# Softmax denominators moved behind V, part of the causal mask moved to TensorE, earlier row maxima and shorter reciprocals in a two-layer transformer kernel

## What is computed

```python
x = x + _L0_attn_ref(_layernorm(x), wq, wk, wv, wo)      # 32 query heads, 8 key/value heads, width 32
x = x + _L0_ffn_ref(_layernorm(x), ...)                  # stream mixing with Sinkhorn
x = x + _L1_attn_ref(_layernorm(x), Wq, Wk, Wv, Wo)      # the same sizes, another rotary order
x = x + _L1_ffn_ref(_layernorm(x), ...)                  # base matrix and experts

# attention:
q = rope(x @ wq); k = rope(x @ wk); v = x @ wv           # each key head serves 4 query heads
scores = q k^T / sqrt(32) + causal mask                  # per head 1024 x 1024
out = softmax(scores) @ v
return out @ wo
```

## Time and profile before

| | |
|---|---|
| median of 3 runs | 3118.09 us (3112.07 to 3120.93) |
| the profiled execution | 3121.41 us, of which its span is 3119.7 us |
| TensorE matmul busy | 2780.3 us, 89% |
| TensorE weight load busy | 1788.4 us, 57% |
| VectorE busy | 1933.4 us, 62% |
| ScalarE busy | 1001.4 us, 32% |
| GpSimd busy | 715.2 us, 23% |
| mean granted clock of TensorE | 0.945 of 2.4 GHz |

### The profile page before, as it was taken

How to read it: one execution, slowest core, us unless ns; L and a number is a source line. 1 busy time by engine, 2 the same in 40 slices (tenths; PEclk the granted TensorE clock), 3 DMA queues, 4 the chain that set the end, 5 groups by cost and what they waited for, 6 DMA issues and landing times. The chain is left out here.

```text
span 3119.7 us, 49191 instructions
## 1 busy us (share of the span) xinstructions
PE 2780.3 (89%) x15824; PEld 1788.4 (57%) x15824; DVE 1933.4 (62%) x4357; ACT 1001.4 (32%) x1549; POOL 715.2 (23%) x693
## 2 busy tenths in 40 slices
PE   7899998999999799652859999989999996997999
PEld 5545554655554488652646455436555542885887
DVE  4577777557777433588765677775677774324543
ACT  2143435134343411352521443433244344101000
POOL 6223231433231000000044323214223220001111
PEclk8999999999999899765979999989999998998999
DMA  3323222323131422000123323223323221443111
GB/s 139 102 64 89 70 72 72 113 73 97 56 102 30 140 81 67 0 0 0 81 115 105 101 63 89 69 64 110 94 63 97 58 77 73 158 135 148 68 67 41
DMA packets 121063, 252.84 MB, mean 81 GB/s; under 512 B 12720, under 2 KB 39728, under 8 KB 120880
## 3 DMA queue, kind: packets, MB, share of 16 engines
q1 hardware_dynamic: 120912, 251.03, 25.5%
HBM read 166.57 MB, written 84.41 MB: 80 GB/s over the span
## 5 line engine op out<-in xcount | busy, mean ns | idle before, releaser
L560 ACT ACTIVATE a_prob<-a_pst 128x1024 f32<-128x1024 f32 (+3 forms) x768 | 593.0, 814 | 726.2 <-PE a_pst L827 724.7
L647 DVE CUSTOM_DVE_ANT_0 a_psh<-a_psh,a_edge 128x128 f32<-128x128 f32 (+3 forms) x1024 | 487.6, 514 | 218.5 <-PE a_psh L780 208.1
L780 PE MATMUL a_psh<-a_kst,a_qst 127*128 127x512 f32 (+3 forms) x1536 | 511.7, 394 | 29.3 <-issue 12.0
L780 PEld LDWEIGHTS a_psh<-a_kst,a_qst 127*128 127x128 f32 x1536 | 255.9, 189 | 455.4 <-DVE a_mx L647 199.3
L827 PE MATMUL a_pst<-a_qst,a_kst 128*128 128x512 f32 (+2 forms) x1536 | 398.8, 361 | 28.9 <-ACT a_prob L560 11.0
L650 DVE TENSOR_REDUCE a_mx<-a_psh 128x1 f32<-128x512 f32 x512 | 343.6, 689 | 71.1 <-PE a_psh L780 65.1
L847 PE MATMUL a_ppv<-a_prob,a_vg 128*32 128x512 f32 (+3 forms) x3072 | 335.0, 508 | 15.6 <-POOL a_prob L464 10.6
L464 POOL TENSOR_SCALAR_AFFINE_SELECT a_prob<-a_prob 128x512 f32<-128x512 f32 x256 | 171.9, 672 | 759.4 <-ACT a_prob L560 758.2
L827 PEld LDWEIGHTS a_pst<-a_qst,a_kst 128*128 128x128 f32 x1536 | 267.1, 192 | 128.4 <-issue 56.2
L847 PE MATMUL a_pden<-a_prob,a_ones 128*32 128x512 f32 (+3 forms) x3072 | 332.0, 504 | 0.0
L691 DVE RECIPROCAL a_dens<-a_dens 128x512 f32<-128x512 f32 x64 | 214.6, 3353 | 75.6 <-ACT a_dens L568 66.4
(11 more groups left out here) (217 smaller groups left out, 3958.8 us busy)
## 6 DMA issues: line engine op xcount, KB each, us to landing
a_qst<-q SPq DMA_DIRECT2D x192, 256.0 KB, 4.5
a_wraw<-in_wqkv SPq DMA_DIRECT2D x52, 512.0 KB, 5.7
q<-a_stg_hi SPq DMA_DIRECT2D x64, 256.0 KB, 2.6
q<-a_stg_lo SPq DMA_DIRECT2D x64, 256.0 KB, 2.8
oT<-a_oT SPq DMA_DIRECT2D x64, 256.0 KB, 2.5
a_kst<-kT SPq DMA_DIRECT2D x96, 128.0 KB, 3.0
h_oraw<-oT SPq DMA_DIRECT2D x16, 512.0 KB, 4.1
h_x<-in_x SPq DMA_DIRECT2D x16, 512.0 KB, 4.7
```

The lines of the kernel that those rows point to most:

```text
L560: act.activation(prob[k % 2][:, 2 * half:2 * half + 2, off:], pst[:, half, :, off:], ACT.Exp, scale=scale).then_inc(s["exp_done"], 1)
L647: part = dve.tensor_tensor_reduce(scores, scores, edge[:, BANK - n:], 1.0, 2 * MASKED, ALU.add, ALU.max, mx_hq[kc][:, h, qt:qt + 1])
L780: mm = pe.matmul(psh[:, at, i * n:(i + 1) * n], qst[par][0:P - 1, h, qt * P:(qt + 1) * P], kst[par][0:P - 1, kc * BANK:kc * BANK + n], sta ...
```

## The change

Six edits, all in the attention.

- `TOGETHER`: in the units 0, 1, 2, 3, 9, 10 and 11, what stood between `("PV", e, 0)` and `("PV", e, 1)` goes behind the latter, so that denominators follow V at once. A use `S` that was due after `("PV", e, 0)` of such a unit goes behind `("ST", e + 1, 1)`, that is, ahead of V.
- The window over which the uses `S` are spread gets two more places ahead: behind `("ST", 1, 1)` and behind `("PV", 0, 1)`. The first use so comes before V of unit 0, and before the last two pieces of the projection.
- Where a use on the diagonal holds more than one head (128 or 256 columns each), TensorE adds the mask with one more matmul per head: a bf16 identity times the last 128 columns of `edge`, accumulated on the scores. VectorE then takes one plain `tensor_reduce` for the whole bank. Uses of 384 and 512 columns stay with VectorE's masked maximum. That is 6 of 38 uses, with 16 matmuls more, per group and per prologue.
- `NORM`: in place of the reciprocal of 128 x 512, VectorE transposes `dens` in blocks of 32 x 32 into `oT[k]`, takes the reciprocal of one column of each block (128 x 16), and transposes that back, repeated, into `dens`. The wait for the store of `oT[k]` moves ahead of the first transpose.
- GpSimd makes the bf16 copy of the identity.
- GpSimd clears the padding of `kst` before the powers, and that of `qst` in eight parts between them.

```diff
+TOGETHER = (0, 1, 2, 3, 9, 10, 11)
...
-        window = [step for unit in steps[1:10] for step in unit]
+        window = [steps[0][1], steps[0][3]] + [step for unit in steps[1:10] for step in unit]
         total, done, k = sum(map(columns, window)), 0, 0
+        slot = {("PV", e, 0): ("ST", e + 1, 1) for e in TOGETHER}
         for step in window:
             done += columns(step)
             while k < len(USES) and k * total < done * len(USES) - total // 2:
-                after[step] += [("S", k)]
+                after[slot.get(step, step)] += [("S", k)]
                 k += 1
...
     order = [("ST", 0, 0), ("ST", 0, 1)] + ([("HI", 1), ("LO", 1), ("RS", 1)] if full_s else []) + first
+    for e in TOGETHER:
+        after["PV", e, 1][:0] = after["PV", e, 0]
+        after["PV", e, 0] = []
...
+        rden = sb("rden", [P, BANK // HD])
...
+            pool.drain()
+            pool.tensor_copy(identb[:, :], ident[:, :])
             pool.drain().then_inc(s["const"], 1)
...
-            for k in range(ST_):
-                reciprocal_deviation(k, k)
-                if k == 5:
-                    w_lo(0, 0)
-            pool.drain()
             for i in range(2):
                 pool.memset(kst[i][96:P, :].bitcast(F32), -1.0)
                 pool.drain()
                 pool.memset(kst[i][96:P - 1, :].bitcast(F32), 0.0)
                 pool.drain()
-                pool.memset(qst[i][96:P - 1, :, :].bitcast(F32), 0.0)
+            for k in range(ST_):
+                reciprocal_deviation(k, k)
+                if k == 5:
+                    w_lo(0, 0)
+                pool.drain()
+                pool.memset(qst[k // GH][96:P - 1, k % GH, :].bitcast(F32), 0.0)
                 pool.drain()
             pool.drain().then_inc(s["padded"], 1)
...
-                if last:
+                if last and m == 1:
...
                         dve.drain()
+                        dve.wait_ge(o_stored[k], DMA0 + n * 16)
+                        dve.sem_inc(s["dve_turn"], 1)
                         dve.wait_ge(s["acc_copied"], AC0 + 2 * q + 2)
-                        dve.reciprocal(dens[:, :], dens[:, :])
+                        dve.transpose(oT[k][:, :], dens[:, :])
                         dve.drain()
-
-                        dve.wait_ge(o_stored[k], DMA0 + n * 16)
+                        dve.reciprocal(rden[:, :], oT[k][:, :].rearrange("p (c r) -> p c r", r=HD)[:, :, 0])
+                        dve.drain()
+                        dve.transpose(dens[:, :], rden[:, :].unsqueeze(2).broadcast_to([P, BANK // HD, HD]))
+                        dve.drain()
                         dve.tensor_tensor(oT[k][:, :], pvs[:, :], dens[:, :], ALU.mult).then_inc(s["norm_done"], 1)
...
                     mm = pe.matmul(psh[:, at, i * n:(i + 1) * n], qst[par][0:P - 1, h, qt * P:(qt + 1) * P],
-                                   kst[par][0:P - 1, kc * BANK:kc * BANK + n], start=True, stop=True,
-                                   skip_group_check=True)
+                                   kst[par][0:P - 1, kc * BANK:kc * BANK + n], start=True,
+                                   stop=not last or len(heads) == 1, skip_group_check=True)
+                    if last and len(heads) > 1:
+
+                        mm = pe.matmul(psh[:, at, (i + 1) * n - P:(i + 1) * n], identb[:, :], edge[:, BANK - P:],
+                                       start=False, stop=True, skip_group_check=True)
```

More of the change, by code:

```diff
@@ L227, in attention @@
         edge = sb("edge", [P, BANK], BF16)
+        identb = sb("identb", [P, P], BF16)
         ones = sb("ones", [P, HD])
@@ L776, in row_scores @@
                 _, at, prev = where
-                qt, kc, n, heads, _ = USES[k]
+                qt, kc, n, heads, last = USES[k]
                 pe.wait_ge(s["sh_free"], SH0 + u + prev + 1)
```

## The result

| | before | changed |
|---|---|---|
| median (lowest to highest) | 3117.15 us (3112.07 to 3120.93), 4 runs | 3151.22 us (3142.90 to 3158.46), 4 runs |
| ratio to before, 95% interval | | 1.0107 [1.0087, 1.0127] |
| the profiled execution, span | 3121.41, 3119.7 us | 3142.90, 3141.2 us |
| mean granted clock of TensorE | 0.945 | 0.947 |

The change makes the kernel 1.1% slower. The forecast was 3146 us; the measured median lies 5 above it and within the range. That it comes so near is in part luck, as the sum further down shows. The four runs of the changed kernel fall in two pairs, 3142.9 and 3144.2, and 3158.3 and 3158.5. The profile belongs to the lower pair, so what it can explain is its own difference of 21.5 us, not the 34 of the medians.

A forecast was written before the change was run, and what follows sets the result against it. TensorE, busy 89% of the span, was taken as the bound. Full groups +26.4, first groups +21.5, setup -12, reciprocals -3.5, rest -4 made +28.4 on the profiled 3121.4; forecast median 3146 us, own range 3130 to 3163, overall 3106 to 3172.

The forecast's parts named there:

- A: Full group, denominators directly behind V: five new joined pairs save 0.31 us each, -1.55 us per full group.
- C: Full group, bank 0 shared by P 0 and S 2: S 2 waits for VectorE's rotate, +1.0 us.
- D: Full group, new waits at S 6, S 35 and S 36 against old waits that mostly go: net +0.1 us.
- B: Full group, 16 mask products on TensorE at 0.097 us each: +1.55 us; bounds 0.053 and 0.3 each.
- E: First group of each batch: TensorE stands at the earlier S 0 for late queries, then low clock; +21.5 us together.
- F: Setup: GpSimd's new padding order removes TensorE's wait for the weights' split at the second projection; -12 us.
- G: End of each attention: short reciprocal with two transposes saves 1.5 to 1.9 us, twice, -3.5; nothing in the groups.
- H: The rest: groups 6 -0.5 us each and prologues -0.5 each, together -4 us.
- VectorE is never late: Rival: C and D's new waits do not arise, full group -0.9 us, 3098 us in all; chance 0.12.
- masks nearly free: Rival: masks cost the low end, half of C is taken up, full group about 0.0, 3120 us; chance 0.15.
- mask products switch the array: Rival: each mask product costs 0.3 us, B becomes 4.8 per full group, 3223 us in all; chance 0.06.
- the early start reaches the queries in time: Rival: first groups' query DMAs are quicker, so E does not arise; 3125 us in all; chance 0.05.

The follow-up runs named there:

- three edits: Changed kernel with P 0 pieces 6 and 7 ahead of S 0, all masks on VectorE, only units 0, 2, 10 newly joined: 3078.17 us, ratio 0.9864.
- late row scores: Changed kernel with the old window, S 0 behind ST 2: 3149.36 us, ratio 1.0088; the same on the three edits: 3093.94 us, 0.9915.

## Why the prediction was right, and where not

**A. Denominators behind V: -1.55 forecast.** The price of a switch was right. A joined pair of unit 1:

```profile
253.24 0.85 PE L865 MATMUL a_ppv<-a_prob,a_vg 128*32 128x384 f32 x8
253.91 0.83 PE L865 MATMUL a_pden<-a_prob,a_ones 128*32 128x384 f32 x8
254.66 0.62 PE L794 MATMUL a_psh<-a_kst,a_qst 127*128 127x384 f32 x2
```

V takes 0.67 and the denominators 0.75 of 0.64 streamed; over five pairs the step distances give 1.38 us against before, 0.28 each where 0.31 was forecast (and 1.18, 0.24 each, against the kernel with the joins undone). What the prediction didn't do was to ask what the join itself makes late. It booked those waits in C and D, apart from A, and took A for a gain. The runs put most of them on the joins: alone, with the row scores behind the pair, +1.1 a group; in the changed kernel +0.17; beside the three edits +0.59 for two more and the row scores that move with them.

**B. Mask products: +1.55 forecast.** Measured: 8 of 128 columns at 0.076 and 8 of the others at 0.09, 1.3 in the changed kernel. The bounds 0.053 and 0.3 were far apart and the nearest row was the right one to take. By the Trainium skill (TensorE: Matmul & The Clock Gate, section "Weight-path perf modes - Fast Weight Load (FWL) and DoubleRow") the estimate was 1.4. The trace agrees on the loads: the identity's is recorded with 0.10 us, that of the queries with 0.20. It agrees less on the split, 0.06 and 0.11 a product estimated against 0.076 and 0.09.

```profile
250.66 0.10 PEld L799 LDWEIGHTS a_psh<-a_edge,a_identb 128*128 128x128 bf16 x1 [0.16 <-issue]
250.66 0.20 PEld L794 LDWEIGHTS a_psh<-a_kst,a_qst 127*128 127x128 f32 x1
```

**C. Rotate's bank: +1.0 forecast.** 1.18 - 0.24 streamed, and 0.1 for exposed weights at S 2: 1.04. The three rows it was built on the earlier trace rows gave it to a few hundredths, and the run that moves P 0 ahead took this away. So did the run without joins and the one with late row scores: it takes both, the join of unit 0 and the early S 2, to bring the wait about.

**D. Other waits: +0.1.** By the step distances ST 3 half 1 takes 0.61 instead of 0.33 ahead of S 6, and S 6 itself some 0.1 more than its columns ask ahead of V: 0.4, as forecast. Around S 35, ST 10 half 1 takes 0.48 instead of 0.33, S 35 0.66 instead of 0.34 and S 36 0.43 instead of 0.33: 0.6 (forecast 0.7). Against them the old waits went only in part. What is left over, 1.20 - (-1.38 + 1.3 + 1.04) = +0.24, is the term, short by 0.14. The group came to +1.20 against +1.1.

**E. First groups: +21.5 forecast, 16.8 measured** beyond the steady +1.2. TensorE stands at S 0 in all four, at the low clock behind it:

```profile
135.95 0.29 PEld L794 LDWEIGHTS a_psh<-a_kst,a_qst 127*128 127x128 f32 x1 [5.97 <-issue]
...
137.53 1.94 PE L865 MATMUL a_ppv<-a_prob,a_vg 128*32 128x512 f32 x8
139.24 1.39 PE L865 MATMUL a_pden<-a_prob,a_ones 128*32 128x512 f32 x8
...
654.58 0.45 PE L794 MATMUL a_psh<-a_kst,a_qst 127*128 127x128 f32 x1 [6.36 <-issue]
1731.57 0.44 PE L794 MATMUL a_psh<-a_kst,a_qst 127*128 127x128 f32 x1 [4.72 <-issue]
2252.00 0.44 PE L794 MATMUL a_psh<-a_kst,a_qst 127*128 127x128 f32 x1 [6.40 <-issue]
```

The eight V products take 1.71 from start to start, where a full group has 0.88. The mis-sized part is the arrival of the queries. S 0 starts 12.3 to 13.2 us behind the group's start in all four; before, it was 14.9 and 14.8 in the first batches and 12.7 and 12.2 in the second. The prediction let the later of these stand, and so put the idle time at 7 to 9 us in all four; it is 4.7 to 6.4. Why the first batches were later before isn't known. The first groups of the kernel with early row scores alone are longer in the same way, by 4.2.

**F. Setup: -12 forecast.** From the prologue's first projection matmul into `pst` to the first group, 92.2 and 92.3 us of before became 84.7 and 84.3. Of this the transposes ahead of it, which start 1.1 us later in layer 1, take a part back: the first group moves from 129.3 to 122.8 in layer 1, and in layer 2 the lag behind before shrinks from 11.7 to 5.0. That is -13.2 with the row maxima. Right in size and place, and TensorE's waits at the second projection no longer name GpSimd.

**G. Reciprocal: -3.5 forecast.** The four operations at the end of attention 1:

```profile
1058.44 0.71 DVE L703 STREAM_TRANSPOSE a_oT<-a_dens 128x512 f32<-128x512 f32 x1 [17.08 <-ACT a_dens L578]
1059.23 0.25 DVE L705 RECIPROCAL a_rden<-a_oT 128x16 f32<-128x16 f32 x1
1059.56 0.71 DVE L707 STREAM_TRANSPOSE a_dens<-a_rden 128x512 f32<-128x512 f32 x1
1060.34 0.69 DVE L709 TENSOR_TENSOR a_oT<-a_pvs,a_dens 128x512 f32<-128x512 f32 x1
```

2.6 us together, as written; TensorE's wait for the next stage's data behind it falls from 16.5 to 15.3, and at the end of attention 2 from 19.9 to 18.7: 2.4 for both, not 3.5. The transpose is like the shuffle. The estimate of 1.24 us for 512 columns of fp32, taken as four times what the Trainium skill (VectorE: DVE Perf Modes, section "The three transpose paths") gives for 128 x 128 bf16, was too high: 0.71 measured. What was missing is group 7 of the first batches, -2.8 each in the changed kernel and -3.4 to -3.8 with the reciprocal alone: that it brings nothing in the groups was said of full groups and taken for all, without following the store of oT through SyncE's queue.

**H. The rest: -4 forecast.** Groups 6 gave -1.8 instead of -2, the prologues of the second batches -0.9 instead of -1. The mixing layer, which the change doesn't touch, was 2.3 longer in the profiled run, and the stages behind attention 2, apart from the wait in G, 1.9 shorter.

The sum in the profiled execution was forecast at +28.4 and came to +21.5: E gave 4.7 less and group 7 another 5.6, while D and the mixing layer took 2 to 3 each. The median still came out above the forecast, since two of the four runs are 15 us above the others. So the mechanisms were right, but that 3146 met 3151 to 5 us is luck: some 10 us of error in E and G met a shift that no trace explains. The rival "VectorE is never late" is refuted by the waits; "masks nearly free" by 1.3 instead of 0.85; "mask products switch the array" by 0.076 to 0.09 each; "the early start reaches the queries in time" by four stalls.

The deeper reading came only with the parts taken alone. In a full group they are +1.1 (joins, with the row scores behind the pair), +1.5 (masks), -0.44 (early start), 0 (reciprocal, setup), which add to +2.2; together they cost +1.2. The joins' own order of row scores is in that difference, so four kernels that all start early compare better (three of them also have the short reciprocal and the new setup, which move no full group):

| with the early start | full group |
|---|---|
| neither joins nor masks (early row scores only) | 52.57 |
| masks (changed, joins undone) | 54.04 |
| joins (changed, masks on VectorE) | 53.18 |
| both (changed) | 54.21 |

Joins alone cost 0.61, masks alone 1.47, both 1.64: the products repair 0.44 of what the joins break, and the step distances find this in the two halves of ST 2, where the joins make VectorE late. In the three edits VectorE is late for 0.2 us of a group by the waits view, with the masks on it, and ST 4 half 0 takes 0.33 more than before; so I take it that the products' 1.3 us would buy back a third of a us at most there. That wasn't run.

## What to carry to other kernels

Closing up two steps that use the array in the same way (here 32 of its 128 columns) saves the cost of going in and out (0.28 us a pair here). But look first at what stood between them. Where it was projections, as in units 0 and 10, the pair was a gain of 0.4. Where it was work that takes turns with another engine on two banks, spacing it out was worth more: in the kernel with joins only, 2.5 us of waits against 1.4 saved. Moving work to the bounding engine pays only where it removes a wait of that engine: the products cost 1.3 us a group and bought back 0.3. And test every part of such a change alone and in pairs: of the five here two are gains alone (reciprocal -0.3%, setup -0.6%), one becomes a gain in company (early start, 0.5% between the two versions of the three edits), and two are losses (masks, and the joins taken as a whole). And look at single groups before taking their mean: two odd ones among 20 turned +0.17 into +0.58.

## What the runs showed of the hardware that I had not expected

- A transpose of 128 x 512 fp32 by VectorE takes 0.711 us on average over 64, little more than a multiplication of that size at its median (0.693).
- The bf16 identity product between fp32 products of the queries costs 0.076 us for 128 columns where the stream alone is 0.053 (0.09 between queries' products of 256 columns); changing the type of the weights between neighbours showed no other price.
- In the kernel with mask products only and in the changed one with late row scores, TensorE stood for 5.5 and 5.8 us at the same place, the start of group 2 (counted from 0) in the first batch of layer 2, and the group after is longer too, by 1.7 and 2.5. None of the other kernels' traces has it. In the first of the two, SyncE took 4.49 us for three key loads that take 1.30 in the groups beside it, which looks like the cause; but in the second the same loads took 1.29. What both traces share is two overlapping transfers of 1.5 to 2.7 us on the queue that the page calls "instruction", some 4 to 5 us ahead of the group's start; at other groups' starts there is none, or a single one of 0.9 to 1.5. Whether these are the cause isn't shown:

```profile
1844.53 4.49 SPq L323 DMA_DIRECT2D a_kst<-kT  x3
...
1850.74 0.79 PE L834 MATMUL a_pst<-a_qst,a_kst 128*128 128x512 f32 x1 [5.51 <-issue]
```

And with late row scores:

```profile
1837.17 1.29 SPq L330 DMA_DIRECT2D a_kst<-kT  x3
...
1844.68 1.64 PE L845 MATMUL a_pst<-a_qst,a_kst 128*128 128x512 f32 x3 [5.77 <-issue]
```
